# Routing inside the first rounds of the shared expert, shared weights kept on chip from the attention stage

## The reference

```python
x = x + attention(layernorm(x), ...)
# in the second half, with xf the 8192 normalised tokens:
logits = layernorm2(xf) @ gate_w.T;  probs = softmax(logits)
tk_probs, tk_idx = top_k(probs, 2);  tk_probs /= sum(tk_probs) + EPS
out = swiglu(xf, sWg, sWu, sWd)            # the shared expert, all tokens
for e in range(8):
    out = out + w[:, e] * swiglu(xf, Wg[e], Wu[e], Wd[e])
x = x + out
```

## Time and profile before

| what | us |
| --- | --- |
| median of 3 runs (2224.26 to 2225.31) | 2224.79 |
| the profiled execution, its own time | 2222.39 |
| its span from first to last instruction | 2220.7 |
| TensorE busy in the span | 1972.8 (89%) |
| VectorE busy | 1252.4 (56%) |
| ScalarE busy | 1081.6 (49%) |
| GpSimd busy | 789.4 (36%) |
| granted TensorE clock, mean | 0.962 |

### The profile page before, as it was taken

The page is one execution under the profiler, slowest core; times in us unless marked ns, Lnnn a source line. Parts: engine busy times, 40 slices in busy tenths (PEclk is TensorE's granted clock), DMA queues, the critical chain, the costliest instruction groups (busy, mean ns, idle before and its releaser), DMA issues. The chain is left out here.

```text
span 2220.7 us, 47761 instructions
## 1 busy us (share of the span) xinstructions
PE 1972.8 (89%) x14698; PEld 1300.3 (59%) x14767; DVE 1252.4 (56%) x3885; ACT 1081.6 (49%) x2354; POOL 789.4 (36%) x1150
## 2 busy tenths in 40 slices
PE   2789999999999999999983699997799999999997
PEld 1345445455444454444432588885577777777776
DVE  5556667766666766667635555552355454544544
ACT  1155555555555555555540455542355555555554
POOL 2033323333333333332330355520244444444443
PEclk9699999999999999999985799998999999999999
DMA  7134343344344344343310565544733333333332
GB/s 211 36 102 113 119 135 122 113 131 118 117 132 128 115 120 122 116 131 119 113 61 15 184 211 207 198 135 156 255 58 58 53 57 55 57 58 54 55 55 36
DMA packets 152032, 246.07 MB, mean 111 GB/s; under 512 B 28896, under 2 KB 90080, under 8 KB 150848
## 3 DMA queue, kind: packets, MB, share of 16 engines
q1 hardware_dynamic: 116352, 189.24, 27.2%
q0 software_dynamic: 32064, 53.44, 11.4%
q10 hardware_dynamic: 3456, 1.34, 0.2%
HBM read 111.89 MB, written 90.50 MB: 91 GB/s over the span
## 5 line engine op out<-in xcount | busy, mean ns | idle before, releaser
L631 DVE CUSTOM_DVE_ANT_0 ps_rows<-ps_rows,maskrow 128x512 f32<-128x512 f32 (+3 forms) x1024 | 484.4, 514 | 304.6 <-PE ps_rows L488 303.7
L576 ACT ACTIVATE probs<-ps_cols 128x512 f32<-128x512 f32 (+3 forms) x1024 | 392.0, 435 | 390.6 <-PE ps_cols L499 383.9
L488 PE MATMUL ps_rows<-ks,qs 32*128 32x512 f32 (+3 forms) x2048 | 426.4, 491 | 88.1 <-DVE mx L631 50.3
L495 PE MATMUL ps_cols<-qs,ks 32*128 32x512 f32 (+3 forms) x2048 | 419.5, 486 | 2.5 <-ACT probs L576 2.4
L1596 POOL DMA_INDIRECT out_dram<-y_e,to x135 | 215.5, 1596 | 369.6 <-DMA out_dram<-y_e,to 193.6
L750 POOL TENSOR_TENSOR pace<-eps 1x1 f32<-1x1 f32 x256 | 58.0, 227 | 781.4 <-ACT probs L576 781.4
L488 PEld LDWEIGHTS ps_rows<-ks,qs 32*128 32x128 f32 x2048 | 161.4, 187 | 296.1 <-DVE mx L631 245.6
L499 PE MATMUL ps_cols<-mT,ones_r 32*128 32x512 f32 (+3 forms) x1024 | 285.3, 551 | 0.0
L1723 DVE TENSOR_TENSOR h_lo<-ps_h,h_hi 128x512 fp32r<-128x512 f32 x135 | 93.3, 691 | 216.1 <-ACT h_hi L1698 215.6
L1692 ACT ACTIVATE sg_e<-ps_ge 128x512 f32<-128x512 f32 x135 | 80.7, 598 | 267.2 <-PE ps_ge L1618 267.2
L512 PE MATMUL ps_o<-probs,vt 128*32 128x512 f32 (+3 forms) x2048 | 192.9, 449 | 0.8 <-POOL probs L752 0.8
(11 more groups left out here) (207 smaller groups left out, 3733.6 us busy)
## 6 DMA issues: line engine op xcount, KB each, us to landing
xs_d<-zrows SPq DMA_DIRECT2D x45, 408.0 KB, 2.9
xr<-xs_d POOLq DMA_DIRECT2D x135, 136.0 KB, 3.1
whi_d<-w_sh SPq DMA_DIRECT2D x16, 768.0 KB, 3.8
w_hi<-whi_d SPq DMA_DIRECT2D x8, 1536.0 KB
xn<-in_L_attn_x_dram SPq DMA_DIRECT2D x16, 512.0 KB, 4.5
ks<-k_lin SPq DMA_DIRECT2D x64, 128.0 KB, 2.8
ks<-k_tan SPq DMA_DIRECT2D x64, 128.0 KB, 3.8
qs<-q_lin SPq DMA_DIRECT2D x64, 128.0 KB, 2.4
```

The lines of the kernel that those rows point to most:

```text
L488: mm = nc.tensor.matmul(ps_rows[bank_of(row_no(g, it, h))][:, 0:(it + 1) * P], qs[at:at + STRIP, d.par, g, it * P:(it + 1) * P], ks[at:at ...
L495: nc.tensor.matmul(ps_cols[bank_of(col_no(n, s, e))][:, jt * P:S], ks[at:at + STRIP, b.par, gc, jt * P:(jt + 1) * P], qs[at:at + STRIP, b. ...
L576: nc.scalar.activation(probs[:, n % 2, 2 * (1 - s) + e, jt * P:S], ps_cols[bank_of(col_no(n, s, e))][:, jt * P:S], ACT.Exp).then_inc(exp_d ...
L631: nc.vector.tensor_tensor_reduce(out=bank, in0=bank, in1=maskrow[:, (TT - 1 - it) * P:S], scale=1.0, scalar=LOWEST, op0=ALU.add, op1=ALU.m ...
```

## The change

The routing and scatter blocks become one block, `front_stage`. TensorE computes the weight sums and turns the logits into the banks of gate and up, transposes batch 0, and starts round 0. VectorE's routing steps are cut into pieces, and between them stands `beside()`, one `vector_unit` of the shared expert: 16 units, those of rounds 0 to 3, lie among the routing steps. The two rank matmuls stand behind unit 0 of round 2, in the banks of the transposes, and TensorE waits for their copies (`rank_taken`) before it transposes in that round. ScalarE computes the exp after its round 0. The clearing of the ring's pads moves from VectorE to GpSimd.

The scatter starts in round 4 (`ROWS_AT`) instead of round 0, with 2, 1, 1 and 2 tiles beside the units instead of 1, 1, 1 and 2, and x1 rows are loaded four batches ahead instead of three.

The shared weights are loaded in the attention stage, behind its first loads, into three tiles that are free until batch 0 (`osb`, `o_val`, `o_inv`). GpSimd splits them there into `swg`, `swu`, `swd`, which stay on chip, 24 KB of each partition, until the shared expert has ended. The first copy into `osb` waits for the split. Loads and splits of the scatter stage go.

```diff
+        with ExitStack() as mid:
...
+            shared = [sbt(mid, name, [P, 2, KT * INTER], F32R) for name in ("swg", "swu", "swd")]
...
+            with nc.cleanup_on_exit(), ExitStack() as c:
+                front_stage(nc, c, sbt, shared, x1_d, out, xs_d, ident, ones, mv2, eps, rstd2, nmr, place, lgT, gws, gwb,
...
+    shared_st = [t[:].rearrange("p a s -> p (a s)") for t in (osb, o_val, o_inv)]
...
         def o_copy(b, g):
             act.wait_ge(pv_done, b.v * STEPS + (g + 1) * TT)
+            if b.off == 0 and g == 0:
+                act.wait_ge(shared_split, 6)
...
+        pool.wait_ge(shared_in, 3 * 16)
+        for m in range(3):
+            nc.gpsimd.tensor_copy(shared[m][:, 0], shared_st[m]).then_inc(shared_split, 1)
+        pool.wait_ge(shared_split, 3)
+        for m in range(3):
+            nc.gpsimd.tensor_tensor(shared[m][:, 1], shared_st[m], shared[m][:, 0].bitcast(F32), ALU.subtract).then_inc(shared_split, 1)
...
+        for m, src in enumerate(shared_weights):
+            sp.dma_start(shared_st[m].rearrange("p (k n) -> p k n", k=IT if m == 2 else KT), src.rearrange("(k p) n -> p k n", p=P))\
+                .then_inc(shared_in, 16)
...
-    def tensor_round(self, pe, s):
+    def tensor_round(self, pe, s, beside=None, before_turn=None):
 
 
         if self.has(s):
             self.gate_up(pe, s, 0)
+            if beside:
+                beside()
             self.gate_up(pe, s, 1)
+            if before_turn:
+                before_turn()
             self.transposes(pe, s.plus(1))
...
+def front_stage(nc, ctx, sbt, shared, x1_d, out, xs_d, ident, ones, mv2, eps, rstd2, nmr, place, lgT, gws, gwb, pos, slot_e):
+
+    FIRST, RING, AHEAD, RANK_AT, ROWS_AT = NB, 8, 4, 2, 4
+    A_ROUND = (2, 1, 1, 2)
 
...
+    ps_l = [bank[:].rearrange("p (b t) -> p b t", t=P) for bank in (*se.ps_g, *se.ps_u)]
+    ps_r, ps_n = (bank[:].rearrange("p (t e) -> p t e", e=NE) for bank in se.ps_t)
+
+    def tiles_of(s, i):
+
+        n = sum(A_ROUND)
+        first = (s.off - ROWS_AT) * n + sum(A_ROUND[:i])
+        many = A_ROUND[i] if s.off < FIRST - 1 else 2
+        return range(max(first, 0), min(first + many, NT)) if s.off >= ROWS_AT else range(0)
...
+        for bt in range(AHEAD):
+            load_rows(bt)
+        loaded = AHEAD
+        for s in range(FIRST + 1):
+            if s >= 1:
+                se.load_in(sp, Batch(0, s + 2))
+            while loaded < NB and (loaded - AHEAD + 1) * TT <= (s - ROWS_AT) * sum(A_ROUND):
+                load_rows(loaded)
+                loaded += 1
+            se.store(sp, Batch(0, s - 1))
+            if s >= 1:
+                se.load(sp, Batch(0, s + 1))
+        for bt in range(loaded, NB):
+            load_rows(bt)
+        for r in range(2):
...
+        def ranks():
+
+            pe.wait_ge(chosen, 1)
+            pe.wait_ge(lower_ready, 1)
+            nc.tensor.matmul(ps_r.rearrange("p t e -> p (t e)"), lower[:], rank[:].rearrange("p t e -> p (t e)"), start=True, stop=True)
+            nc.tensor.matmul(ps_n.rearrange("p t e -> p (t e)"), ones[:], rank[:].rearrange("p t e -> p (t e)"), start=True, stop=True)\
+                .then_inc(ranked, 1)
+
+        def ranks_taken():
+            pe.wait_ge(rank_taken, 1)
+
+        se.transposes(pe, Batch(0, 0))
+        for s in range(FIRST + 1):
+            if s == RANK_AT:
+                se.tensor_round(pe, Batch(0, s), ranks, ranks_taken)
+            else:
+                se.tensor_round(pe, Batch(0, s))
...
         act.wait_ge(v3_ready, 1)
         nc.scalar.activation(rr[:], v3[:], ACT.Sqrt, bias=eps[:, 0:1]).then_inc(root, 1)
-        act.wait_ge(exp_in, 1)
-        nc.scalar.activation(prob[:], a[:], ACT.Exp).then_inc(exp_out, 1)
+        se.copies(act, Batch(0, 0))
+        for s in range(FIRST + 1):
+            se.scalar_round(act, Batch(0, s), norm_rows)
+            if s == 0:
+                act.wait_ge(exp_in, 1)
+                nc.scalar.activation(prob[:], a[:], ACT.Exp).then_inc(exp_out, 1)
...
+        for q in range(RING):
+            nc.gpsimd.memset(row[q][:, :, D:XW], 0.0).then_inc(cleared, 1)
...
-    @block.gpsimd
-    def _(pool):
+        pool.wait_ge(pos_ready, 2)
...
+        def beside():
+
+            s, i = divmod(units[0], IT)
+            units[0] += 1
+            se.vector_unit(dve, Batch(0, s), i)
+            if i == IT - 1 and se.has(Batch(0, s)):
+                se.lower(dve, Batch(0, s), IT - 1)
...
+        dve.wait_ge(root, 1)
+        then(nc.vector.reciprocal(rstd2[:], rstd2[:]))
+        then(tt(v3[:], mv2[:, :, 1], rstd2[:], ALU.mult))
+        tt(v3[:], v3[:], rstd2[:], ALU.mult).then_inc(v3_ready, 1)
+        se.norm(dve, Batch(0, 0))
+        nc.vector.scalar_tensor_tensor(out=nmr[:], in0=mv2[:, :, 0], scalar=-1.0, in1=rstd2[:], op0=ALU.mult, op1=ALU.mult)
+        nc.vector.memset(one64[:], 1.0)
+        dve.wait_ge(sums_ready, 1)
+        nc.vector.tensor_copy(sgb[:], ps_s)
+        dve.wait_ge(turned, 1)
...
+        se.lower_rows(dve, Batch(0, 0))
+        se.norm(dve, Batch(0, 1))
+        dve.wait_ge(root, 2)
+        then(nc.vector.reciprocal(rr[:], rr[:]))
+        then(tt(rr[:], rr[:], rstd2[:], ALU.mult))
+        then(nc.vector.tensor_copy(m1[:], mv2[:, :, 0]))
+        beside()
+        then(tt(a[:], over_e(m1[:]), over_t(sgb[:, 0]), ALU.mult))
+        then(tt(a[:], logits[:], a[:], ALU.subtract))
+        then(tt(a[:], a[:], over_e(rr[:]), ALU.mult))
+        beside()
+        then(tt(a[:], a[:], over_t(sgb[:, 1]), ALU.add))
+
+        then(nc.vector.tensor_reduce(m1[:], a[:], AX.X, ALU.max))
+        tt(a[:], a[:], over_e(m1[:]), ALU.subtract).then_inc(exp_in, 1)
+        beside()
+        beside()
+        dve.wait_ge(exp_out, 1)
+        then(nc.vector.tensor_reduce(m1[:], prob[:], AX.X, ALU.add))
+        then(nc.vector.reciprocal(m1[:], m1[:]))
+        then(tt(prob[:], prob[:], over_e(m1[:]), ALU.mult))
+        dve.wait_ge(iotas, 3)
+        beside()
+
+        def choose(p, best, onehot):
+
+            then(nc.vector.tensor_reduce(best[:], p[:], AX.X, ALU.max))
+            then(tt(a[:], p[:], over_e(best[:]), ALU.is_equal))
+            then(tt(a[:], a[:], over_t(desc[:]), ALU.mult))
+            beside()
+            then(nc.vector.tensor_reduce(cc[:], a[:], AX.X, ALU.max))
+            then(tt(onehot[:], over_t(desc[:]), over_e(cc[:]), ALU.is_equal))
...
+        beside()
+        assert units[0] == RANK_AT * IT
+
+        then(tt(cc[:], m1[:], m2[:], ALU.add))
+        then(nc.vector.tensor_scalar(cc[:], cc[:], EPS, None, ALU.add))
+        then(nc.vector.reciprocal(cc[:], cc[:]))
+        then(tt(place[:, :, 0, 1], m1[:], cc[:], ALU.mult))
+        then(tt(place[:, :, 1, 1], m2[:], cc[:], ALU.mult))
+        beside()
+        dve.wait_ge(ranked, 1)
+        nc.vector.tensor_copy(b[:], ps_n)
+        then(nc.vector.tensor_copy(rank[:], ps_r))
+        nc.vector.nop(nofuse=True).then_inc(rank_taken, 1)
+        for e in range(NE):
+            s_ = nc.vector.tensor_tensor_scan(a[:, :, e], one64[:], b[:, :, e], 0.0, ALU.mult, ALU.add)
+        then(s_)
+        beside()
+        then(nc.vector.tensor_copy(tot[:], a[:, NT - 1]))
...
+        beside()
...
+        for r in range(2):
+            then(tt(a[:], rank[:], oh[r][:], ALU.mult))
+            then(nc.vector.tensor_reduce(cc[:], a[:], AX.X, ALU.add))
+            nc.vector.tensor_copy(pos[:, :, r], cc[:]).then_inc(pos_ready, 1)
+            dve.wait_ge(pos_ready, r + 1)
+            beside()
+        then(tt(cmp_[:], start[:].unsqueeze(2).to_broadcast([1, NSLOT, NE]),
+                incl[0:1].unsqueeze(1).to_broadcast([1, NSLOT, NE]), ALU.is_ge))
+        beside()
+        then(nc.vector.tensor_reduce(cnt[:], cmp_[:], AX.X, ALU.add))
+        then(nc.vector.tensor_scalar(slot_e[:], cnt[:], float(NE - 1), None, ALU.min))
+        while units[0] < (FIRST + 1) * IT:
+            beside()
 
 
```

Of what goes, the loads and the order of the scatter stage (the routing steps themselves are the same):

```diff
-    FIRST, RING, AHEAD = NB, 8, 3
-    A_ROUND = (1, 1, 1, 2)
...
-        se.load_weights(sp)
-        se.load_in(sp, Batch(0, 1))
-        for b in range(AHEAD):
-            load_rows(b)
-        se.load(sp, Batch(0, 0))
-        se.load(sp, Batch(0, 1))
-        se.load_in(sp, Batch(0, 2))
-        loaded = [AHEAD]
-
...
-    @block.tensor
-    def _(pe):
-        se.transposes(pe, Batch(0, 0))
-        pe.wait_ge(se.w_lo, 3)
-        rounds(lambda s: se.tensor_round(pe, s))
```

More of the change, by code:

```diff
@@ L1204, in sem @@
         return nc.alloc_semaphore(name)
+    row = [sb(f"row{q}", [P, 2, XW]) for q in range(RING)]
+    xw = sb("xw", [P, AHEAD, TT, D])
     rr = sb("rr", [P, NT])
@@ L1227, in route_stage @@
     logits = sb("logits", [P, NT, NE])
[L1228 to L1231 removed]
+    cleared = sem("cleared")
+    xw_loaded = [sem(f"xw_loaded{r}") for r in range(AHEAD)]
+    normed = sem("normed")
+    scattered = [sem(f"scattered{q}") for q in range(RING)]
     filled = sem("filled")
@@ L1283, in _ @@
                        allow_small_or_imprecise_dtypes=True).then_inc(iotas, 1)
```

(13 more changed lines are left out.)

203 lines of the change are left out of this document (58 added, 145 removed).

## The result

On the chip on which the change was first measured, the changed kernel takes 2201.39 us (median of four, 2198.30 to 2204.30) against 2224.53 for the kernel before: 0.9894 of it, with a 95% interval of 0.9878 to 0.9909. It is faster, by 23 us, where 41.6 were forecast; 2201.4 lies outside the range of 2177 to 2197. The profiled execution took 2203.89 us.

The account below looks back on a forecast made before the run. Bound by one VectorE chain, then a load, up to the first gate, and by TensorE in the rounds. 46.6 + 2.3 - 2.0 - 4.1 - 0.5 - 0.7 = 41.6 us gained; forecast 2183.2 us, range 2177 to 2197.

Parts of the forecast that it names:

- First gate: Shared expert's first gate product moves from 1241.07 to 1194.5 us, 8 us after the block's first instruction: 46.6 us gained.
- TensorE's waits in the first rounds: Routing in VectorE's queue makes TensorE wait 1.45 us on the rank sum and 2.65 before round 2's transposes: 4.1 lost.
- rival 1: First rounds: VectorE's queue hides routing less well, 9.7 us exposed instead of 4.1, up to 7 more; 2189 to 2196; chance 0.19.
- rival 4: First rounds: routing hidden better, TensorE's waits fall to nothing; 2177 to 2179 us; chance 0.10.
- Table changes: ScalarE, rounds 0 and 1: loading the Exp and then the Silu table, 1.28 us each, is hidden by 0.25 and 0.4.
- rival 3: ScalarE's table changes take twice as long and delay the routing's choice and rank sum by 2.2 us; 2185.4; chance 0.07.
- The clock: Full clock from the first gate to round 4's down product, instead of 1.2 GHz at first: 2.3 us gained.
- rival 2: TensorE's waits in rounds 0 to 2 lower the clock for one round: about +15 us, 2198; chance 0.06.
- The border with its clearing: Before the experts start, the block now clears its semaphores on exit: 0.7 us lost.
- The start: Loading the shared weights, 1.5 MB, in the attention stage delays the first row products: 0.5 us lost, range 0 to 2.
- the paragraph on the scatter: Rounds 4 to 14: twelve indirect DMAs, 15.1 to 16 us of a 17.54 us round, are hidden, the last in round 14.
- The end of the attention: Attention ended at 1186.24 us before; an end later than 1188 was named as a sign of a wrong prediction.

Follow-up runs that it names:

- e5: Changed kernel unaltered, as a control on another chip than the first: 2181.00 us, 0.9794 of the kernel before.
- e6: Kernel before, unaltered, as the second control: 2226.09 us.
- e11: Changed kernel unaltered again, on one more chip: 2180.14 us, 0.9800 of the kernel before.
- e12: Changed kernel unaltered again, on the chip of e3 and e4: 2183.19 us, 0.9814 of the kernel before.
- e4: Changed kernel with each scatter DMA moving 16 numbers of a row's 272, routed experts working on zero rows: 2175.46 us.
- e7: Kernel before with only the row tiles changed, to 2, 1, 1, 2 beside a round's units: 2225.45 us, 1.0012 of the kernel before.
- e10: Kernel before with the tie (second output and third Silu wait by program for scattered rows to land): 2229.32 us, 1.0020 of the kernel before.
- e13: Changed kernel with five row tiles a round, begun one round earlier, on the chip of e12: 2180.52 us.
- e8: Changed kernel with the tie: second output and third Silu wait by program until the second unit's rows have landed; 2196.77 us, 0.9858 of before.
- e9: Changed kernel with five row tiles a round, begun one round earlier, and the same tie as e8: 2177.42 us, 0.9775 of the kernel before.
- e16: Changed kernel unaltered, one execution on a later chip: 2203.99 us against 2226.40 for the kernel before.
- e3: Changed kernel with the 128 scatter DMAs replaced by no-operations, routed experts working on zero rows: 2175.59 us.

## Why the prediction was right and wrong

**The sum was right where the hold-back is absent.** On the chip of e5 and e6, one profiled execution each, the pieces are (us):

| piece | before (e6) | changed (e5) | difference | forecast |
|---|---|---|---|---|
| block's first instruction | 1187.83 | 1190.10 | +2.3 | +0.5 |
| from there to the first gate | 54.9 | 7.8 | -47.2 | -46.6 |
| to the fourth round's down product | 73.1 | 74.2 | +1.1 | +3.8 |
| from there to the experts' first load | 215.2 | 217.3 | +2.1 | +0.7 |
| all, with 0.3 less behind it | 2226.09 | 2184.16 | -41.9 | -41.6 |

The forecast of 2183.2 stands beside medians of 2181.0, 2180.1 and 2183.2. That this one pair comes within 0.3 us of the 41.6 is partly luck: waits of TensorE that were 2.7 us shorter than forecast stand against an attention part that ended later and a clock that fell at the end, together 3.3 us more than forecast. By the medians the change brings 42.7 us on this chip, 45.6 and 42.8 on the two others. Terms, one by one:

- First gate: 7.7 to 7.8 us after the block's first instruction, where 8 had been named. The normalisation begins 3.4 us after it instead of 3.9.
- TensorE's waits in the first rounds: 1.47 us, not 4.1. The wait on the rank sum didn't occur: VectorE finished `rank` at 1230.85 and TensorE came for it at 1231.44. So VectorE's queue hid the routing better than forecast; rival 1 fell, and rival 4 was half right.
- Rank matmuls: the two pairs take 1.87 us together at the full clock, 2.0 had been taken.
- Table changes: rival 3 fell. In the lines above the first load of 1.28 us starts 0.02 us after the activation before it has ended, the second 0.03, and the exponential 0.01 us after the load. (The Trainium skill, ScalarE: Activation LUTs, What ACT_TABLE_LOAD costs, adds a drain of 1.38 us: no such gap stands here, so its 2.66 us would be twice too much.)
- The clock: full from the first gate on; rival 2 fell. The stretch to the down product of round 4 got 2.3 us shorter by it, as forecast; the matmuls that ran at the lower level before were 11 (in 1241.07 to 1245.70), not the 22 of the prediction, on which the sum doesn't rest. What I hadn't seen is a fall at the other end: in e5, e11 and e12 the last down product takes 7.5 us instead of 6.0. Whether the change has a part in it is open. Of the eleven executions of the changed kernel and its variants without hold-back or tie ten have it (e4 hasn't), of the three of the kernel before without a tie (the first, e6, e7) none; but e10, the kernel before with the tie, has it, and the first chip's changed kernel hasn't. Between e6 and e5 it is 1.5 of the 2.1 us in the table's fourth row. In e11 (columns: length, TensorE busy and instructions, its weight loads, VectorE, ScalarE, GpSimd, granted clock, DMA share, GB/s):

```profile
1474.00:1477.00 3.00, 2.14 (x12) 2.15 (x13) 0.70 (x2) 0.08 (x1) 0.00 (x0) 0.73 0.00 0
1477.00:1479.00 2.00, 2.00 (x12) 2.00 (x12) 0.00 (x0) 0.00 (x0) 0.00 (x0) 0.55 0.00 0
1479.00:1481.00 2.00, 2.00 (x19) 2.00 (x18) 0.69 (x1) 0.00 (x0) 0.00 (x0) 1.00 0.00 0
```

- The border with its clearing: 3.27 us from the last output to the experts' first load instead of 2.67, so 0.6; 0.7 had been taken.
- The start: the DMA share in 30 to 41 us rose from 0.44 to 0.81, and the first row products come at 57.7 to 59.1 us in the sixteen executions with the changed part, at 57.8 to 59.1 in the four with that of before. No cost can be told from the spread.

**The failed step is the paragraph on the scatter.** It called twelve indirect DMAs, 15.1 to 16 us in a round of 17.54, "hidden", and took for granted that both kernels have the same 17.54 us a round from the fifth on. The cost of one was right (954 ns shortest, 960 median, 1592 longest). The last one started at 1484.0, in round 15, whose first gate product is at 1481.32, and not before it. What was wrong is the kind of test: I compared a busy time with the round, as for an engine that only has to keep up. On a chip with the hold-back GpSimd stands in a loop with ScalarE and VectorE, and the links count: 2.3 us from the release to its first scatter, 14.7 from there to its twelfth, 2.8 from that to the next release, 19.8 us. For five tiles I estimate 2.5 less, two times 1.265, so 17.3, just inside the round. "Wrong, if rounds 4 to 14 are longer than 17.6" named the place, but no rival gave it a price.

The row that could have told me was in my hands. I read "8.4 us after the down product's start" out of the earlier trace rows and used it as a property of the down product ("the late second half"), two words away from "<-remote". The rounds of the same trace without row tiles have 6.04. A releaser that is no engine, on an output that only needs TensorE, was the hold-back, and the one thing that the change was going to lengthen was the run that it follows.

**The end of the attention.** It came 5.2 us later in the profiled execution of the changed kernel, against the 0.5 forecast and the 1188 named as a limit. The shared weights alone don't explain this. In sixteen executions with the changed kernel's attention part the block's first instruction lies between 1182.0 and 1191.7 us, in four with the part of before between 1182.1 and 1187.8. The granted clock differs between them. Two stretches of before and of the changed kernel (columns as above), and the second of e6, the kernel before on another chip:

```profile
150.00:160.00 10.00, 8.34 (x66) 3.45 (x65) 5.60 (x21) 3.37 (x10) 2.64 (x6) 0.67 0.24 68
160.00:170.00 10.00, 8.61 (x98) 4.35 (x98) 7.05 (x29) 5.32 (x15) 4.64 (x10) 1.00 0.57 185
```

```profile
150.00:160.00 10.00, 8.34 (x66) 4.07 (x66) 5.47 (x22) 2.63 (x8) 2.64 (x6) 0.60 0.24 76
160.00:170.00 10.00, 9.13 (x56) 3.39 (x51) 4.78 (x16) 3.86 (x9) 2.97 (x6) 0.55 0.49 158
```

```profile
160.00:170.00 10.00, 9.13 (x56) 3.39 (x52) 4.66 (x16) 3.74 (x9) 2.97 (x6) 0.55 0.46 150
```

From 150 to 160 the granted clock is low for a time in all three; in the second ten it is full in the first execution and mostly at the lower level in the other two, one of either kernel. The unaltered changed kernel's times on chips without the hold-back spread over 2173.6 to 2186.0; such falls may make that much, though not every one is traced. Executions with equal clocks end their attention part nearly alike. With a mean granted clock of 0.91 in 140 to 180 us and 0.92 in 1000 to 1180, the first kernel before ends it at 1186.3 and eight executions of the changed part at 1186.1 to 1187.9. With 0.79 and 0.94, e6 and e7 end it at 1187.8 and 1186.8 and e13 at 1187.1. The five latest, 1190.1 to 1191.7 and the first chip's changed kernel among them, have 0.79 and 0.93; all five are of the changed part, so a share of the change in such an execution isn't excluded. What decides between the levels is open.

**What stays open.** Why TensorE's semaphores are raised late on some chips. The release follows the last bytes of the scatter by 0.7 to 0.8 us in the changed kernel and by 0.0 to 0.5 in the kernel before, while its distance from GpSimd's last start varies by 0.12 and 0.14 us; this speaks, weakly, for the issuing rather than the bytes, but neither thin rows nor five tiles of the changed kernel could be tried on such a chip, so it isn't settled. A rival that no run tests is the recording itself. All four executions with the hold-back lack semaphore records (24,451 to 24,896), all fifteen others with the full scatter or thin rows have 26,586 to 26,596. Every execution on record, profiled or not, comes with a span and a granted clock, so no run here is known to be free of recording.

That a loop of this kind costs 16.6 us with six tiles and nothing with five is shown by e8 and e9. That the chip's own hold-back is that loop rests on the same links (19.46 and 19.81 us), on the fixed distance to the end of GpSimd's run, and on the kernel before, which has five tiles and the hold-back and keeps its rounds of 17.55. Five tiles a round from one round earlier lose nothing where six lose nothing, and kept their rounds under the tie but for the first two; it is the version I would take, though on a chip with the hold-back it was not measured.

## What to carry to other kernels

A helper engine that is busy 15 of 17.5 us is hidden only if nobody waits for it in turn: where its first work waits for a result and a result waits for its last, add the links and compare the loop with the round. When the profile names a releaser that makes no sense for the instruction, compare the same instruction in rounds without the suspect before using its time as a property. And before explaining experiments that all cure the same fault, run the unaltered kernel beside them on the same chip.

## What the runs showed of the hardware

- The same program can have VectorE and ScalarE held back behind a GpSimd scatter on some chips and not on others. The changed kernel's second output came 11.0 to 12.7 us after the down products' start in the first measurement and in e16; it came at 6.04 us in every round with row tiles of the thirteen executions without the tie on four other chips (e3, without the scatter, among them).
- With the hold-back TensorE's semaphore for the second output was raised up to 6.6 us after the recorded end of its last matmul (first measurement), without it 0.01 us after (e12), and some 1700 to 2150 of 26,600 records of semaphores are missing from the traces with it.
- A run of indirect DMAs issued without a gap beside TensorE doesn't by itself delay the others: 6.04 us in e4, e5, e11 and e12.
- One fall of the granted clock ended before 160 us in one execution and well behind it in another with the same attention part (the first kernel before and e6: 1.00 and 0.55 in 160 to 170 us).
